# Two causal attentions: the mask moves from TensorE into VectorE's row-maximum pass

## The reference, cut to what matters

```python
# first attention (head width 16), per batch and head
s = jnp.einsum('bhqd,bhkd->bhqk', q, k) / math.sqrt(DH) + alibi + mask   # mask: -inf above the diagonal
p = jax.nn.softmax(s, axis=-1)
o = jnp.einsum('bhqk,bhkd->bhqd', p, v)
# second attention (head width 64, rotary embedding), likewise
att = jnp.where(tril, q @ k.T * scale, -inf); y = softmax(att) @ v
```

## Time and profile before

| what | value |
|---|---|
| time, median of 3 runs | 2404.24 us (2403.8 to 2404.24) |
| the profiled execution, its own time | 2399.85 us |
| its span | 2398.0 us |
| mean granted TensorE clock | 0.939 |
| first attention, first to last scores | 54.1 to 639.6 us |
| second attention, first to last scores | 1024.4 to 2062.3 us |

### The profile page before, as it was taken

The page is one execution under the profiler, slowest core; times in us unless marked ns, Lnnn a source line. Parts: engine busy times, 40 slices in busy tenths (PEclk is TensorE's granted clock), DMA queues, the critical chain, the costliest instruction groups (busy, mean ns, idle before and its releaser), DMA issues. The chain is left out here.

```text
span 2398.0 us, 56553 instructions
## 1 busy us (share of the span) xinstructions
PE 2014.5 (84%) x18246; PEld 1457.5 (61%) x18247; DVE 1731.8 (72%) x3603; ACT 1470.1 (61%) x2926; POOL 1032.3 (43%) x1226
## 2 busy tenths in 40 slices
PE   3999999999862997487898989989898999739999
PEld 2766766666561665155666767666666767525665
DVE  3877777777792443477687777869597886579997
ACT  1867766677562444186677676858587787434443
POOL 4534533345004000589655465747465574032222
PEclk8999999999956999699999999999999999959999
DMA  6000000000033332012100000000000000100000
GB/s 232 2 2 0 0 0 0 0 0 1 2 118 131 104 86 74 4 15 36 15 2 3 2 3 2 2 2 2 3 2 3 2 2 2 37 1 13 15 17 25
DMA packets 53114, 57.64 MB, mean 24 GB/s; under 512 B 7120, under 2 KB 47216, under 8 KB 52896
## 3 DMA queue, kind: packets, MB, share of 16 engines
q1 hardware_dynamic: 46240, 45.00, 6.1%
q0 software_dynamic: 6656, 9.85, 2.0%
HBM read 36.22 MB, written 18.61 MB: 23 GB/s over the span
## 5 line engine op out<-in xcount | busy, mean ns | idle before, releaser
L1028 ACT ACTIVATE prob_sb<-a_bank,neg_max_sb 128x128 f32<-128x128 f32 (+3 forms) x512 | 256.5, 529 | 159.7 <-DVE neg_max_sb L1107 146.6
L1107 DVE TENSOR_REDUCE neg_max_sb<-a_bank 128x1 f32<-128x128 f32 (+3 forms) x512 | 237.2, 486 | 142.2 <-PE a_bank L896 135.9
L371 PE MATMUL a_bank<-w_in_sb,xnT_sb 128*128 128x512 f16 x1152 | 293.4, 393 | 29.0 <-DVE t_buf_sb L579 20.6
L531 DVE TENSOR_REDUCE neg_max_sb<-a_bank 128x1 f32<-128x128 f32 (+3 forms) x512 | 235.7, 481 | 110.7 <-PE a_bank L288 109.9
L434 ACT ACTIVATE prob_sb<-a_bank,neg_max_sb 128x128 f32<-128x128 f32 (+3 forms) x512 | 259.1, 537 | 57.6 <-DVE neg_max_sb L531 54.8
L442 ACT ACTIVATE p_hi_sb<-a_bank 128x384 f16<-128x384 f32 (+1 forms) x384 | 204.5, 533 | 116.3 <-PE a_bank L297 115.2
L538 DVE TENSOR_TENSOR p_lo_sb<-a_bank,p_hi_sb 128x384 f16<-128x384 f32 (+1 forms) x384 | 227.6, 594 | 52.7 <-ACT p_hi_sb L442 50.4
L453 ACT ACTIVATE stack_sb<-a_bank 128x1024 f16<-128x1024 f16 (+1 forms) x256 | 209.7, 820 | 45.1 <-PE a_bank L342 43.4
L297 PE MATMUL a_bank<-ident_f_sb,prob_sb 128*128 128x128 f32 x1280 | 208.2, 278 | 0.6 <-ACT prob_sb L434 0.6
L707 POOL TENSOR_TENSOR rope_w_sb<-t_buf_sb,sin_sb 128x256 f32<-128x256 f32 x128 | 125.0, 976 | 185.5 <-DVE t_buf_sb L579 183.6
L909 PE MATMUL a_bank<-ident_f_sb,prob_sb 128*128 128x128 f32 x1280 | 204.4, 274 | 0.1
(11 more groups left out here) (253 smaller groups left out, 5524.3 us busy)
## 6 DMA issues: line engine op xcount, KB each, us to landing
sorted_rows<-zeros_sb SPq DMA_DIRECT2D x1, 4992.0 KB, 21.8
x_in_sb<-sorted_rows SPq DMA_DIRECT2D x39, 128.0 KB, 2.2
sorted_results<-y_moe_sb SPq DMA_DIRECT2D x39, 128.0 KB, 1.7
x_sb_sb<-L_attn_x SPq DMA_DIRECT2D x8, 512.0 KB, 10.7
w_raw_sb<-L_ffn_gate_bank SPq DMA_DIRECT2D x8, 512.0 KB, 4.1
w_raw_sb<-L_ffn_up_bank SPq DMA_DIRECT2D x8, 512.0 KB, 5.0
w_raw_sb<-L_ffn_down_bank SPq DMA_DIRECT2D x8, 512.0 KB, 6.3
out<-x_sb_sb SPq DMA_DIRECT2D x32, 128.0 KB, 1.7
```

What stands on the lines that cost most here:

```text
L371: last = pe.matmul(out, xnT[:, x, c, j * P:(j + 1) * P], w["in"][:, w_, c, cols], start=k == 0, stop=k == len(terms) - 1)
L531: last = dve.tensor_reduce(neg_max[:, i:i + 1], S[(3 * h + g) % 2][:, off:off + L], AX.X, ALU.max, negate=True)
L1028: last = act.activation(prob[g][:, h % 2, off:off + L], S[(3 * h + g) % 2][:, off:off + L], ACT.Exp, bias=neg_max[:, i:i + 1])
L1107: last = dve.tensor_reduce(neg_max[:, i:i + 1], S[(3 * h + g) % 2][:, off:off + L], AX.X, ALU.max, negate=True)
```

## The change

The mask matmuls go. `mask` becomes 128 x 512 (bf16): a row block of L columns uses its last L columns, 0 where allowed and -1e30 above the diagonal. VectorE runs one fused pass per row block in place of the reduction: it reads scores from PSUM and mask from SBUF, writes -(score + mask) to `prob` in SBUF, and gives the row minimum of that, which is the negated maximum. A one-element memset goes ahead of each group's passes. The exponential then reads and writes `prob` in SBUF (scale -1). Waits move with it: the scores of a group wait for `s_max`, no longer for `s_exp`, of the group two back; `row_max` takes over exp's wait on the transposes, and in the first attention also waits for exp three groups back.

```diff
@@ attention, scores
-            wait(pe, s_exp, G - 1)
+            wait(pe, s_max, G - 1)
...
-                    pe.matmul(out, q, stack[:, h % 2, 2 * T:2 * T + L], start=False, stop=False)
+                    last = pe.matmul(out, q, stack[:, h % 2, 2 * T:2 * T + L], start=False, stop=True)
...
-                last = pe.matmul(out[:, L - P:L], ident_b[:, :], mask[:, :], start=False, stop=True)
@@ attention, exp
-            wait(act, s_pt, G - 2)
...
-                last = act.activation(prob[g][:, off:off + L], S[(3 * h + g) % 2][:, off:off + L], ACT.Exp, bias=neg_max[:, i:i + 1])
+                p = prob[g][:, off:off + L]
+                last = act.activation(p, p, ACT.Exp, bias=neg_max[:, i:i + 1], scale=-1.0)
@@ attention, row_max
+            wait(dve, s_pt, G - 2)
             wait(dve, s_scores, G + 1)
+
+            dve.memset(mark[:, (3 * h + g) % 4:(3 * h + g) % 4 + 1], 0.0)
...
-                last = dve.tensor_reduce(neg_max[:, i:i + 1], S[(3 * h + g) % 2][:, off:off + L], AX.X, ALU.max, negate=True)
+                last = dve.tensor_tensor_reduce(prob[g][:, off:off + L], S[(3 * h + g) % 2][:, off:off + L],
+                                                mask[:, T - L:T], -1.0, BIG, ALU.add, ALU.min, neg_max[:, i:i + 1])
@@ attention0, row_max (scores and exp as above)
+            wait(dve, s_exp, G - 2)
+            if g == 0:
+                wait(dve, s_pt, 3 * (b * HEADS + h - 1))
             wait(dve, s_scores, G + 1)
```

More of the change, by code:

```diff
@@ L26 @@
 NEG = -1.0e30
+BIG = 3.0e38
 DH0 = D // HEADS
@@ L159, in attention @@
     neg_max = sb(f"neg_max{layer}", [P, QT], F32)
+    mark = sb(f"mark{layer}", [P, 4], F32)
     y = sb(f"y{layer}", [P, 2, QT, P], F32)
@@ L794, in attention0 @@
     neg_max = sb("neg_max0", [P, QT], F32)
+    mark = sb("mark0", [P, 4], F32)
     oT = sb("oT0", [P, T], F32)
@@ L893, in scores @@
                 L = (i + 1) * P
-                out = S[(3 * h + g) % 2][:, off:off + L]
-                pe.matmul(out, stack[0:K0, h % 2, i * P:(i + 1) * P], stack[0:K0, h % 2, T:T + L], start=True, stop=False)
-                last = pe.matmul(out[:, L - P:L], ident_b[:, :], mask[:, :], start=False, stop=True)
+                last = pe.matmul(S[(3 * h + g) % 2][:, off:off + L], stack[0:K0, h % 2, i * P:(i + 1) * P],
+                                 stack[0:K0, h % 2, T:T + L], start=True, stop=True)
                 off += L
@@ L1022, in exp @@
             wait(act, s_max, b * GROUPS + 3 * h + g + 1)
-            if g == 0:
-                wait(act, s_pt, 3 * (b * HEADS + h - 1))
             off = 0
@@ L1027, in exp @@
                 L = (i + 1) * P
-                last = act.activation(prob[g][:, h % 2, off:off + L], S[(3 * h + g) % 2][:, off:off + L], ACT.Exp, bias=neg_max[:, i:i + 1])
+                p = prob[g][:, h % 2, off:off + L]
+                last = act.activation(p, p, ACT.Exp, bias=neg_max[:, i:i + 1], scale=-1.0)
                 off += L
@@ L1106, in row_max @@
                 L = (i + 1) * P
-                last = dve.tensor_reduce(neg_max[:, i:i + 1], S[(3 * h + g) % 2][:, off:off + L], AX.X, ALU.max, negate=True)
+                last = dve.tensor_tensor_reduce(prob[g][:, h % 2, off:off + L], S[(3 * h + g) % 2][:, off:off + L],
+                                                mask[:, T - L:T], -1.0, BIG, ALU.add, ALU.min, neg_max[:, i:i + 1])
                 off += L
@@ L2200, in build @@
         x_sb = sb("x_sb", [P, N_TILES, D], F32)
-        consts = {k: sb(k, [P, P], dt) for k, dt in
-                  (("ident_f", F32), ("ident_b", BF16), ("ident_h", F16), ("mask", BF16))}
+        consts = {k: sb(k, [P, n], dt) for k, n, dt in
+                  (("ident_f", P, F32), ("ident_b", P, BF16), ("ident_h", P, F16), ("mask", T, BF16))}
         stats = {"bn": sb("bn", [P, N_TILES, 6], F32), "mv": sb("mv", [P, N_TILES, 2], F32),
@@ L2319, in host_constants @@
          "tile_no": np.broadcast_to(np.arange(SLOTS, dtype=np.float32), (P, SLOTS)),
-         "mask": np.where(np.arange(P)[None, :] > np.arange(P)[:, None], NEG, 0.0).astype(bf)}
+         "mask": np.where(np.arange(T)[None, :] - (T - P) > np.arange(P)[:, None], NEG, 0.0).astype(bf)}
     start = 2 ** (-2 ** (-(math.log2(HEADS) - 3)))
```

## The result

| | before | changed |
|---|---|---|
| time, median of 5 runs each | 2403.8 us (2401.07 to 2404.24) | 2415.57 us (2411.48 to 2423.46) |
| ratio | 1 | 1.0057, 95% interval 1.0039 to 1.0074 |

The change costs some 12 us where I had forecast 11 less. The time lies in my range, but the sign is wrong. The changed kernel also scatters more, and its profiled execution is the slowest of its five (2423.46 us, span 2421.4), so rows of it are set against the medians with care.

What follows compares the result with a forecast made beforehand. PE was taken as main bound of both attentions, with DVE bounding or level in eleven of 32 heads. Terms -24 + 14 - 16 + 12 + 3 = -11 gave 2393 us against the median 2404.24; range 2360 to 2428.

Steps and rivals of the forecast that it cites:

- (d): First attention: row maximum now waits for two transposes issued behind the scores; 0.07 us in a third of 128 heads, +3 us.
- The sum by heads: Both attentions: PE's mask savings less DVE's added work, head by head; -13 us in the first, -11 in the second, -24 together.
- small instructions: DVE, both attentions: four read-outs and three memsets a head at 0.07 us each, 0.49 us a head.
- Rival 3: DVE: each read-out waits for its pass to end, 1.25 us more a head, 2474 us; chance 0.17 shared with a slower pass.
- (b): Both attentions: PE no longer waits for exp, only for the row maximum; half the relief counted, -16 us.
- the ring: PE's scores waiting for exp before the change: 3.9 us in 480 in the first attention, 20.9 in 780 in the second.
- (a): Eleven heads bound by DVE: half of their present DVE idle time stays, 1.7 us a batch, +14 us.
- head rule: Each head: no shorter than DVE's busy time + 0.49 us; where DVE is no bound, its length less PE's share.
- (c): DVE's queue: copies behind a row maximum come 0.14 to 0.28 us later and PE waits for them, +12 us.
- (e): ACT: exp reads SBUF instead of PSUM, 0.02 us x 1024 = 23 us more of ACT, covered by its slack.
- (f): Start of the kernel: a mask table four times as large is loaded once under the other loads, costing nothing.

Runs made afterwards that it cites:

- e2: Kernel before, with only the first attention's row maximum of a head's first group also waiting for the transposes two heads back: 2425.29 us, ratio 1.0093.
- e1: Changed kernel with four `prob` buffers per group in the first attention in place of two, so row maxima wait for older transposes: 2398.15 us, ratio 0.998.
- e7: e1 with the scores of both attentions waiting for exp again, as before the change: 2395.57 us, ratio 0.9973.
- e6: Kernel before without the mask matmuls, so no causal mask in the diagonal blocks: 2388.67 us, ratio 0.9941.
- e13: Kernel before with each row maximum taken over the first 128 columns of its block only: 2367.04 us, ratio 0.9854.
- e14: Kernel before without mask matmuls and with row maxima over 128 columns only: 2337.62 us, ratio 0.9736.
- e8: Kernel before with the change in the second attention alone, exp there reading unmasked scores from PSUM and scores waiting for exp: 2385.67 us, ratio 0.993.
- e12: Kernel before with 96 unused matmuls ahead of the second attention's loop: 2390.35 us, ratio 0.9958.

## Why the prediction was wrong

**The step that failed is (d), the row maximum's wait for transposes.** I put it at +3 us; e2 measures 22.3 and e1 17.4. I read the delay off one head in which DVE had slack, took it for 0.07 us, and let it cost in a third of the heads. It is 0.29 us in the head above, and against e1 it is 0.3 to 0.4 us in ten heads of 16 and 0.9 in one. I had let the row maximum start with the recorded end of the transposes. It starts 0.22 us behind it: the transposes end at 242.25, and the trace has two more instructions of VectorE's queue, each for a wait, at 242.29 and 242.36, ahead of the memset at 242.47. I also priced the wait by itself and not by its queue: every copy behind it is late too, PE waits for one of them 0.48 us longer in the head above, and then its clock can fall.

In the first head of batches 2 to 6 the row maximum is later still, but not by this wait. Timeline of DVE there before, in the changed kernel, and in e7, which needs no fresh transposes (the first scores start at 194.31, 195.65 and 192.92):

```profile
194.80 0.62 DVE L1107 TENSOR_REDUCE neg_max_sb<-a_bank 128x1 f32<-128x128 f32 x2 [1.28 <-PE a_bank L896]
```

```profile
197.59 0.06 DVE L1113 MEMSET mark_sb<- 128x1 f32 x1 [2.63 <-PE a_bank L915]
```

```profile
194.66 0.06 DVE L1113 MEMSET mark_sb<- 128x1 f32 x1 [2.43 <-PE a_bank L915]
```

The row maximum starts 1.94 us after the first scores, 1.74 in e7, and 0.49 before. What holds it is VectorE's own turn of the loop. In the trace its branch ends at 194.25 in the changed kernel, and the next register instruction of its queue starts at 197.25, 3.00 us later (2.7 to 3.0 over the five turns, in e7 too, and 3.5 to 3.8 in e2), where it is 0.3 us in the kernel before. It costs little in the changed kernel: the first head takes 5.41 to 5.67 us there and 5.05 in batch 1, which stands behind no turn, 2.2 us in all. Why a few more instructions on VectorE bring it about, no run here shows.

**The sum by heads, -24, was too good.** It is added up rightly from its rule. It took PE's 0.24 and 0.225 us as a gain in 21 of 32 heads, because DVE is not full there. Without the wait (e1, e7) the first attention gains 3 to 7 us where the rule said 13; the second gains 0 where it said 11. e6, e13 and e14 show why for the second attention: a window's busy time says whether an engine is full over a head, not whether PE already waits for a copy of it inside. In the heads where PE does wait, its saved time only lengthens the wait. The gain is real only where PE is full: the five heads of the second attention in which PE has no gap before (3, 4, 8, 10, 14) get 0.18 to 0.48 us shorter, three of them from 6.61 to 6.36, and others give it back (7.08 to 7.39, 7.63 to 7.91).

**The small instructions cost less than 0.49 us a head.** The read-out does not wait for its pass: at 242.51, 242.73 and 243.07 above, two passes with their read-outs take 0.56 us from start to the next instruction, where two reductions took 0.54. Each read-out starts 0.07 or 0.08 us before its pass has ended, and together with the instruction behind it. The memset takes 0.04 us where DVE had waited (242.47 to 242.51). DVE busy of 614.05 us against 613.57 in the second window says the same. Rival 3 is refuted for this pass. The rule of the Trainium skill that stood behind it ("VectorE: DVE Perf Modes", "The DRAIN you can't avoid") has an exception in the same section, which I had left out: a next instruction that is not held starts earlier. That fits the 0.07 to 0.08 us of this trace. So the loss had to be looked for in waits.

**(b), -16 for the ring, was worth nothing that shows in the time** (e7). I had misread its row: of the 20.9 us in the earlier trace rows, 9.8 are four waits of 2.35 to 2.55 us at the turn of the loop, which the change does not touch, and only 11 are the ring. Of these, 5.1 became waits for the row maximum and 2.8 waits for exp at the transposes behind the scores, which need the same exp. **(a)**, +14 for DVE idle, was a guess on the same head rule and falls with it. **(c)**, things behind the row maximum later, had the right kind: the second attention's wait for `y` grows by 6.8 us in 780. But e6, with no instruction added to DVE, shows 31.5 too: so it is at least as well explained by PE arriving earlier as by DVE being later. **(e)** holds: exp at 512 columns takes 722 ns and took 695, and e7 against e8 shows no cost of it. **(f)** holds: the first scores start at 54.3 us, and at 54.1 before. The 3.0 us between the two attentions were in no term, and no run says where they come from.

**What I did not see at all** is the turn of the second attention's loop, 10 us and more that depend on the place of the code. It was in the profile of before as a clock of 0.97 in the earlier trace rows. Both kernels lie badly, so it makes no difference between them, but it went into (b) as exp's, and it bears on every experiment that changes TensorE's code.

## What to carry to other kernels

When a wait moves from an engine with slack to one whose queue others wait on, price it over every position of the schedule where the producer stands late, and with all that queues behind it. Work taken from one of two engines that wait for each other is worth what it is worth after the other has been relieved; a two by two of kernels that leave work out shows it for the price of three runs. A wait that comes once a turn of a loop and is much longer than its neighbours may be the turn's, whatever the profile names: here that held for half of the exp waits. And before comparing versions of a looped program within 1%, compare the same instructions with some padding ahead of the loop.

## What the runs showed of the hardware that I had not expected

- The read-out of a fused pass's minimum takes 80 to 83 ns and starts together with the next instruction, 0.07 to 0.08 us before its pass has ended; the pass at 512 columns takes 684 to 686 ns, as the plain reduction does (688).
- A gap of PE of 1.31 us was followed by 1.2 GHz in four of six batches and by 2.4 GHz in two, with the same instructions; 0.83 us in that place (before) and 0.87 (e1, e7) never were. A gap of 1.07 us in head 15 was followed by it in five of six batches in e1, and one of 1.06 in none in e7.
- 32 or 96 unused matmuls ahead of a loop made a 2400 us kernel 8 and 12 us faster. At a turn PE stopped twice before, 2.4 us ahead of the first slot and 2.2 us inside it, and for long only once in e12, 2.8 us ahead of it.
- VectorE's queue went on 0.3 us after its loop's branch in the first attention before, 2.7 to 3.0 us after it with the fused passes, and 3.5 to 3.8 us after it in e2, which adds one wait a head.
